# A causal attention and routed feed-forward kernel: the decay block becomes the stationary operand of the value products, and buffers are laid out anew between its two stages

## The reference, cut to what matters

```
pos_emb = rpe[hops]                                  # 512 x 512 rows of the table
k_hop = jnp.einsum('bhvc,vmhc->bhvm', qh, pe)
qk = jnp.einsum('bhsd,bhtd->bhst', qh, k_scaled)
D = jnp.exp(log_D - max_log_D)                       # causal decay
C = (qk + k_hop) * D
Cn = C / (normalizer + EPS)
h = Cn @ vh
hn = (h - mu) / jnp.sqrt(var + LN_EPS)
...
x = x + xattn(layernorm(x), ctx); x = x + ffn(layernorm(x))
```

## Time and profile before

| | us |
|---|---|
| median of 3 executions | 3314.08 |
| lowest and highest | 3312.99, 3314.81 |
| time of the profiled execution | 3310.51 |
| its span in the profile | 3308.5 |
| end of the last hop product (TensorE) | about 1325 |
| first scores | about 1361 |

### The profile page before, as it was taken

How to read it: one execution, slowest core, us unless ns; L and a number is a source line. 1 busy time by engine, 2 the same in 40 slices (tenths; PEclk the granted TensorE clock), 3 DMA queues, 4 the chain that set the end, 5 groups by cost and what they waited for, 6 DMA issues and landing times.

```text
span 3308.5 us, 69970 instructions
## 1 busy us (share of the span) xinstructions
PE 2938.0 (89%) x24660; PEld 1856.5 (56%) x24660; DVE 2417.6 (73%) x5103; ACT 1941.4 (59%) x4654; POOL 2023.2 (61%) x2195
## 2 busy tenths in 40 slices
PE   6777777777777777699999999999999999999998
PEld 4555454544544554366666666666666666666664
DVE  5655555555555555588888888888888888888875
ACT  3444444444444444477666676666766767667663
POOL 6777777777777777256455455564554645546554
PEclk8888899999999999799999999999999999999999
DMA  9999999999999999556556565565565655656542
GB/s 283 345 349 349 320 348 344 344 352 352 347 345 346 351 348 326 190 184 189 180 174 185 178 189 179 177 187 181 177 190 169 195 173 179 187 179 180 185 148 66
DMA packets 414909, 799.98 MB, mean 242 GB/s; under 512 B 107338, under 2 KB 213834, under 8 KB 412516
## 3 DMA queue, kind: packets, MB, share of 16 engines
q1 hardware_dynamic: 312516, 453.08, 43.6%
q0 software_dynamic: 82560, 270.60, 24.5%
q10 hardware_dynamic: 19488, 71.84, 5.6%
HBM read 618.02 MB, written 176.69 MB: 240 GB/s over the span
## 4 chain that ended last, share of the span: by engine, by line
PE 65%; DMA 16%; POOL 9%; issue 5%; DVE 4%; ACT 1%; SPq 0%; POOLq 0%; DVEq 0%; ACTq 0%
DMA arena<-in_L_xattn_rpe_dram,arena 15%; PE psum L1772 13%; PE psum L1689 9%; PE psum L1701 9%; PE psum L1724 9%; PE psum L1627 7%; PE psum L1600 6%; POOL arena L797 6%; PE psum L1616 4%; PE psum L1753 3%; PE psum L1776 3%; PE psum L1664 2%; POOL arena L782 2%; PE psum L1569 1%; DVE arena L1237 1%
## 5 line engine op out<-in xcount | busy, mean ns | idle before, releaser
L797 POOL DMA_INDIRECT arena<-in_L_xattn_rpe_dram,arena x768 | 731.8, 953 | 235.0 <-issue 181.6
L1600 PE MATMUL psum<-arena 128*128 128x128 f32 x4128 | 614.4, 297 | 190.3 <-DMA arena<-in_L_xattn_rpe_dram,arena 178.6
L1600 PEld LDWEIGHTS psum<-arena 128*128 128x128 f32 x4128 | 488.9, 151 | 422.9 <-DMA arena<-in_L_xattn_rpe_dram,arena 292.9
L993 ACT ACTIVATE arena<-arena 128x512 f32<-128x512 f32 (+3 forms) x1024 | 496.3, 555 | 43.7 <-PE psum L1724 39.2
L1772 PE MATMUL psum<-arena 128*128 128x512 f32 x1024 | 493.3, 595 | 0.0
L1347 DVE TENSOR_TENSOR arena<-psum,arena 128x1024 f32<-128x1024 f32 (+1 forms) x384 | 386.6, 1041 | 133.3 <-PE psum L1701 122.4
L573 DVE COPY arena<-psum 128x512 f32<-128x512 f32 x384 | 263.4, 689 | 239.3 <-PE psum L1600 235.5
L582 DVE COPY arena<-psum 128x416 f32<-128x416 f32 (+15 forms) x512 | 225.3, 442 | 278.4 <-PE psum L1616 270.1
L823 POOL TENSOR_SCALAR_AFFINE_SELECT arena<-arena 128x256 f32<-128x256 f32 x256 | 118.7, 464 | 503.9 <-ACT arena L993 491.6
L1616 PE MATMUL psum<-arena 64*32 64x416 f32 (+7 forms) x8192 | 361.5, 422 | 59.3 <-ACT arena L909 38.1
L573 ACT COPY arena<-psum 128x512 f32<-128x512 f32 x384 | 225.8, 588 | 251.7 <-PE psum L1600 248.7
(11 more groups left out here) (112 smaller groups left out, 4632.1 us busy)
## 6 DMA issues: line engine op xcount, KB each, us to landing
arena<-in_x_dram SPq DMA_DIRECT2D x256, 256.0 KB, 4.1
arena<-gate_rows SPq DMA_DIRECT2D x128, 512.0 KB, 4.4
arena<-in_x_dram SPq DMA_DIRECT2D x512, 64.0 KB
arena<-in_ctx_dram SPq DMA_DIRECT2D x32, 1024.0 KB, 7.5
out_dram<-arena SPq DMA_DIRECT2D x128, 256.0 KB, 2.9
arena<-in_L_xattn_rpe_dram,arena POOLq DMA_INDIRECT x1032, 7.1
arena<-hop_products SPq DMA_DIRECT2D x128, 128.0 KB, 2.6
arena<-hop_products SPq DMA_DIRECT2D x128, 120.0 KB, 2.5
```

Source lines behind the costliest of these rows:

```text
L797: nc.gpsimd.indirect_dma_start(out=rows[set_of(n, v)][:, t, :], out_offset=None, in_=rpe[:, :], in_offset=bass.IndirectOffsetOnAxis(ap=her ...
L993: last = nc.scalar.activation(decay[u % DECAYS][:, e, at:at + width], top_pair[p % 2][:, e * S + j * P:e * S + j * P + width], ACT.Exp, bi ...
L1600: last = nc.tensor.transpose(turn_bank(o)[:, q * P:(q + 1) * P], own[:, q * P:(q + 1) * P], ident)
```

## The change

It does four things.

1. `weigh` swaps the operands. The stationary operand is now one 128 x 128 block of the decay matrix, the moving operand the 64 columns of values, and the result stands with the queries on the rows. `pair_turned`, `turn_back` and the buffer `attT` go. One run of `RUNS` becomes one matmul for each block and head.
2. The stage buffers are placed anew (`place_in`), so that the context and queries of batch 0 can be loaded in the hop stage, behind group 124 of 128, and `hop_in[0]` can be cleared by GpSimd before that stage ends.
3. `hops_over` no longer waits for the stores. Those waits stand at the places that need them (`products_stored`). Before the first scores SP loads both hop buffers, the second one ahead of the context of batch 1 and of the store of the gate rows.
4. In the first round the turn of the gate statistics stands behind the first scores.

```diff
@@ weigh @@
-                    for n, (j, at, width) in enumerate(RUNS[k]):
-                        for e in range(HPT):
-                            last = nc.tensor.matmul(psum[e * DH:(e + 1) * DH,
-                                                         pair_bank(p) * BANK + j * P:pair_bank(p) * BANK + j * P + width],
-                                                    values[ra.par][:, j, HPT * p + e, :],
-                                                    decay[u % DECAYS][:, e, at:at + width],
-                                                    start=(k == 0 and n == 0), stop=True, skip_group_check=True)
+                    out = bank(pair_bank(p)).rearrange("p (i e c) -> p i e c", i=ST, e=HPT)
+                    for j, at, width in RUNS[k]:
+                        for n in range(width // P):
+                            for e in range(HPT):
+                                last = nc.tensor.matmul(out[:, j + n, e, :],
+                                                        decay[u % DECAYS][:, e, at + n * P:at + (n + 1) * P],
+                                                        values[ra.par][:, j, HPT * p + e, :],
+                                                        start=(k == 0 and n == 0 and e == 0), stop=True,
+                                                        skip_group_check=True)
                     last.then_inc(pe_a.sem, pe_a.step(("value", u)))
-
-                def turn_back(r, p):
-                    pe.wait_ge(act_o.sem, act_o.done(r.b, ("turned", p)))
-                    turn(pair_bank(p), attT).then_inc(pe_o.sem, pe_o.step(("back", p)))
@@ hop stage, SP @@
+                if n == GROUPS - 4:
+                    sp.wait_ge(*pe_h.at(("prod", GROUPS // 2 - 1, VG - 1)))
+                    sp.wait_ge(lists_ready, LISTS * len(LIST_ORDER))
+                    load_context(Round(0, 0))
+                    load_queries(Round(0, 0))
@@ hops_over @@
-            for c in range(QUARTERS):
-                engine.wait_ge(hop_stored[c], 32 * (GROUPS // QUARTERS + 1))
@@ round, SP @@
                 if rp and not ra:
-                    load_context(rp)
-                    load_queries(rp)
-
-                    sp.wait_ge(dve_setup, 9)
                     sp.wait_ge(pool_setup, 4)
-                    for i in ((0, 1), (2, 3)):
-                        load_hop(rp, 0, i)
-                if ra:
+                    products_stored(sp, GROUPS // 2)
+                    load_hop(rp, 0, (0, 3))
+                    products_stored(sp, GROUPS)
+                    load_hop(rp, 0, (1, 2))
+                if ra and rf:
                     load_hop(ra, 1, (0, 1))
                     load_hop(ra, 1, (2, 3))
...
+                if rp and not ra:
+                    sp.wait_ge(pool_setup, 5)
+                    load_hop(rp, 1, (0, 1))
+                    load_hop(rp, 1, (2, 3))
@@ GpSimd @@
+            pool.wait_ge(*pe_h.at(("prod", GROUPS - 1, 0)))
+            nc.gpsimd.memset(hop_in[0], 0.0).then_inc(pool_setup, 1)
             hops_over(pool)
-            nc.gpsimd.memset(hop_in[1], 0.0).then_inc(pool_setup, 1)
@@ TensorE, first double @@
+                    if ra and not rf and d == 0:
+                        gate_stats(ra)
                     if d == 0:
-                        if rf:
-                            turn_back(rf, 3)
@@ ScalarE @@
                 if ra:
-                    pair_turned(ra, 0)
+                    pair_out(ra, 0)
```

More of the change, by code:

```diff
@@ L207, in build @@
         mgate_sum = place(DIM)
[L210 to L225, removed]
@@ new lines, in build, with place_in @@
+        hop_zone += [(rows_at + i * KEPT, rows_at + i * KEPT + 2 * DIM) for i in range(ROW_SETS)]
+        hop_zone += [(diag_at + HPT * CAUSAL, after_hops_small)]
+        out_zone = [(after_hops_small, ARENA)]
+        def place_in(zones, n):
+            for zone in zones:
+                for i, (first, end) in enumerate(zone):
+                    if end - first >= n:
+                        zone[i] = (first + n, end)
+                        return arena[:, first:first + n]
+            assert False, n
@@ new lines, in build @@
+        early, late = [hop_zone], [out_zone, hop_zone]
+        context = arena[:, rows_at:rows_at + ROW_SETS * KEPT].rearrange(
+            "p (i t d) -> p i t d", i=ROW_SETS, t=ST - 1)[:, 0:ST, 2, :]
+        xq = [rows[ST + i][:, 2, :] for i in range(2)] + [hopsT[:, 2 + i, :] for i in range(2)]
+        hop_in = [arena[:, diag_at:diag_at + HPT * CAUSAL], place_in(late, HPT * CAUSAL)]
+        hop_in = [h.rearrange("p (e c) -> p e c", e=HPT) for h in hop_in]
+        values = [place_in(early, ST * DIM).rearrange("p (t h c) -> p t h c", t=ST, h=NH) for _ in range(2)]
@@ new lines, in build @@
+        qT = [place_in(zone, KT * S).rearrange("p (k s) -> p k s", k=KT) for zone in (early, late)]
+        kT = [place_in(zone, KT * S).rearrange("p (k s) -> p k s", k=KT) for zone in (early, late)]
+        att = [place_in(late, ST * DIM).rearrange("p (t h c) -> p t h c", t=ST, h=NH) for _ in range(2)]
+        att_sq = place_in(late, ST * HPT * VC).rearrange("p (t e c) -> p t e c", t=ST, e=HPT)
+        decay = [place_in(early, HPT * 4 * P).rearrange("p (e c) -> p e c", e=HPT) for _ in range(DECAYS)]
@@ new lines, in build @@
+        top_pair = [place_in(early, HPT * S) for _ in range(2)]
+        g_z, g_m, g_l, g_c, g_zi, g_rows, g_ctx = [place_in(early, S) for _ in range(7)]
+        g_i = g_l[FG:GR, :]
+        xq_norm = [place_in(early, DIM) for _ in range(2)]
+        x_res = [place_in(late, DIM) for _ in range(2)]
+        att_w = place_in(late, DIM).rearrange("p (h d) -> p h d", h=NH)
+        x1 = [place_in(late, DIM) for _ in range(2)]
+        x1_b = [place_in(late, DIM) for _ in range(2)]
+        ffn_x = place_in(late, DIM)
@@ L524, in build, with products_stored @@
         block = ctx.enter_context(nc.Block())
+        def products_stored(engine, groups):
+            for c in range(QUARTERS):
+                engine.wait_ge(hop_stored[c], 32 * (groups // QUARTERS + 1))
         def hops_over(engine):
@@ L546, in batch_loop @@
             body(0, -1, "np")
+            products_stored(engine, GROUPS)
             body(0, 0, "npa")
```

90 lines of the change are left out of this document (38 added, 52 removed).

## The result

The changed kernel takes **3517.54 us** (median of 3, 3517.20 to 3519.23), the kernel before 3314.08. The ratio is 1.0616, with a 95% interval of 1.0601 to 1.0630. It is slower by 203 us. The forecast was 3495 in a range of 3455 to 3535. The side and the cost of the value products were right. A wait in the rounds, the passage and the first rounds were not, and the loss was put 22 us too small.

The account below looks back on a forecast made before the run. TensorE was taken to bound the rounds. To the profiled 3310.5 us came +192 (rounds), -5 (first groups), -1 (tail) and -5 (passage), giving 3491.5; that execution was 3.6 under the median, so 3495 us, range 3455 to 3535.

Parts of the forecast that it names:

- the passage: From hop stage to first scores: VectorE starts 10.3 us sooner, delays take part back; net -5 us, between -11 and +3.
- the first rounds: From 1361.30 to 1431.52, where TensorE idles 10.2 us: of 9 us of added products, 5 count as hidden.
- Never waits: In the full rounds TensorE never waits, busy 1735.74 of 1738.29 us, so its program sets the kernel's time.
- The pace of a load: Value products: each short matmul costs its 128-column load, 0.110 us, so 160 take 17.6 us a round for 9.53.
- The rivals with hidden and half hidden loads: Value products: loads hide, 3239 us, chance 8%; or part hides, 0.075 to 0.100 each, 3316 to 3444, chance 6%.
- The upper bound: Value products: at most 0.12 us per matmul, the start-to-start time of L1753 with the same load shape.
- the top case: Value products at the full 0.12 us pace: 51 us more, 3546 us.
- So no new wait should appear in a full round: Full rounds: other engines do the same or less in 65.9 us for 59.9, so no new wait.
- so I add nothing: Passage: batch 1's context waits behind the 16 hop loads, but its turns come after the first exponentials, so no cost.
- The 3 us in the queue: Passage: the gate rows' store goes about 3 us late behind 16 hop loads in the SP queue.
- The +2 for early loads: Hop stage: 2 MB of context and queries loaded at 1280 to 1325 compete with the gathers, +2 us.
- the rival: Rounds: short streaming drops TensorE's granted clock to 0.96, 88 us more, 3583 us; chance 6%.

Follow-up runs that it names:

- second version of experiment 5: Changed kernel with the value products of unit 4 moved ahead of the turn of the fourth query tile in double 2: 3507.17 us, ratio 1.0564.
- experiment 1: Changed kernel with the old value products, copies and turns back; new buffers and passage kept: 3315.14 us, ratio 1.0005 to the kernel before.
- experiment 2: Kernel before with the swapped value products alone, no turns back, old passage and buffers: 3516.34 us, ratio 1.0606.
- Experiments 3 and 4: Changed kernel streaming 32 of 64 value columns (3609.37 us), loading half the decay columns (3300.86) or streaming 128 (3522.10); then streaming 48 (3528.92).

## Why the prediction was nearly right, and where it was short

**What bounds the kernel: right, but for a word.** TensorE's program in the rounds set the time in every version; its waits there never came to more than 21.1 us in 29 rounds. "Never waits" was not quite so before either: two waits make 1.7 us, and with them the rounds took 1.8 us more than 29 x 59.88.

**The pace of a load: right.** 0.110 us was put, 0.111 measured. The step from four score loads to 160 decay loads held, and the halving of loads and the doubling and halving of streams show that it is the load. In the chain the groups are 17.53 us for the predicted 17.3, +0.23 in a round or +7 in 29. The rivals with hidden and half hidden loads are out. The upper bound, though, was worked out wrong: by the row shown, (1.18 - 0.28) / 7 is 0.129 and not 0.12, and the top case 3592 and not 3546. Other groups of eight of L1753 last 1.11 us, which gives 0.119. The 0.055 for 64 streamed columns was an estimate from those rows; the version with halved loads, where a matmul of that width starts each 0.059, shows only that it is not more than that. That the two heads' score loads go side by side is in the trace: at 2033.06 they start 0.007 us apart, and the next two 0.11 behind them.

**The turns back, "So no new wait should appear in a full round": the step that failed.** The four turns were counted as 1.76 us saved. One of them, back 0 in double 2, stood where TensorE would otherwise have waited for ScalarE's copies. It took 0.44 us and its loss saves only 0.10; the other 0.34 return as a wait, 29 times, 9.7 us in all. The second version of experiment 5 takes them away and brings 66.42 to 66.08. A wait of TensorE for ScalarE in the rounds was one of the prediction's own signs of being wrong, and it came. For the 29 rounds the forecast was 13.8 us short. The wait (9.9 as 29 x 0.34) and the pace (7) make about 17. Against that stand the 1.8 us by which the rounds before were longer than counted, and 1.1 that stay open.

**The passage, "so I add nothing" for the context: wrong.** The 3 us in the queue were right: the store left 3.4 us behind the scan (L1349) that it waits for. The sum left out that the megabyte of context now stood directly ahead of the small store, 0.44 us and not 4.7 as before. Its round trip took 5.5 us for 1.5. From the end of the last hop product to the first exponential it is 36.5 us for 39.6, so 3.1 less, where -10.3 + 3 would be 7.3. The hop stage itself ended 2.5 us later, at 1327.8, and so the first exponential was level with before. The +2 for early loads is not shown by that: the stage ended at 1324.1 in experiment 1, which has them, and at 1328.1 in experiment 2, which has not.

**The first rounds: a term was missing.** I counted 9 us of products, 5 of them hidden. From the first value group to the gate products of the third batch, before, in the changed kernel and in experiment 2 (columns as in the earlier trace rows):

```profile
1369.20:1431.52 62.32, 53.25 (x392) 34.49 (x393) 46.27 (x77) 43.41 (x99) 21.52 (x32) 1.00 0.63 193
1368.61:1443.38 74.77, 70.60 (x516) 59.78 (x517) 46.99 (x78) 43.14 (x98) 23.58 (x34) 0.89 0.53 158
1373.44:1448.35 74.91, 68.09 (x516) 57.79 (x516) 46.76 (x79) 43.26 (x98) 23.31 (x34) 0.93 0.54 161
```

The hidden part was right: TensorE idles for 4.2 us in this stretch and not 9.1. The products were nearly right: nine groups less five turns back are 12.0 - 2.2 = 9.8 us at the full clock. But TensorE is busy for 17.4 us more. The other 7.5, by this estimate, are the clock, 0.89 for 1.00, and the forecast had no such term.

Where the clock was low is known. The early scores leave a gap in front of the first value products. TensorE stands idle for an activation of ScalarE (L1099, 5.6 us), for the context (7.9) and for a copy (L994, 5.3), and the stretch from 1351 to 1376 has a mean granted clock of 0.50, the lower of the only two values, 0.50 and 1.00, that the clock's records of this case hold. The first value group took 7.06 for 3.68 us, the scores behind it 2.82 for 1.56. In experiment 2, where the scores stand directly ahead, that group takes 3.76, and the stretch from 1373.40 to 1377.10 has a clock of 1.00. But there the clock falls later, a group of 32 behind a wait of 2.5 us takes 6.37 (clock 0.56 from 1424 to 1430), and the whole stretch takes 74.9 us all the same. So it is shown that the order of the scores moves the low clock, not that it would save its cost. Passage and first rounds were -1 by the forecast and +11.9 by the profile.

**The clock in the rounds.** It did not fall, so the rival is out for this kernel. The runs of turns that spoke against it are in the trace of the kernel before: L1701 and L1627 from 2019.08 to 2022.45, 28 rows in 3.37 us, in a stretch at 1.00. Experiments 3 and 4 show that the rival was a real one.

**The range.** The time lies in it, in part by luck. Its upper end was put above a slower pace, 0.117. The pace was 0.111, and what used the room was a wait, a slow round trip and a low clock, from none of which that end was worked out.

## What to carry to other kernels

Before swapping the operands of a float32 matmul, count the loads and their columns: here each of the two loads and matmuls that one makes cost 0.111 us with 128 columns of weights, whether it streamed 32, 64 or 128 columns, and 0.059 with 64 columns of weights and 64 streamed, and a round's value products took 17.53 us with the 128-column operand stationary and 9.53 with the 64-column one. So here the narrow operand belonged on the stationary side. An instruction that is removed from the engine that sets the time saves its duration only if the next one there is ready (here 0.44 us of turns saved 0.10); read what stood behind it and on which copy that waits. Here a small store on the critical path came back some 3 us later (5.5 for 2.4) when it was issued right behind a large load, so its turn in the queue is not all that counts.

## What the runs showed of the hardware that was not expected

- Less work took longer: with 32 of 64 columns streamed in the value products the mean granted clock of the rounds was 0.95, and they took 88 us more; with 48 it was 0.99 and 11 us more; with 64 and 128 columns it was 1.00.
- A 16 KB store was read back 5.5 us after its issue when a 1 MB load had been issued 0.44 us before it, 2.4 us after when 16 loads of 8 to 128 KB stood ahead, and 1.5 us after when the 1 MB load had gone out 4.7 us before.
- The pace of the weight loads did not depend on what the matmuls between them streamed: 0.111 us with 32, 64 and 128 columns.
- Behind eight rows of router products, the first value product of a group started 1.04 us after the first of them when its loads had 64 columns, and 0.94 us when they had 128.
